# A node's own row in a graph adjacency: summed by products with a unit matrix, or counted into the adjacency itself

## What is computed

```python
# L0: h = x + sum over edges of x[src];  two dense layers, relu
# L1: four times:  h = h @ W;  sum over edges AND the node itself
loop = jnp.arange(n);  src = concatenate([edge_index[0], loop]);  dst = concatenate([edge_index[1], loop])
agg = segment_sum(h[src] * (dinv[src] * dinv[dst])[:, None], dst)
# L2: h = nfeat @ Wn + bn;  msg = edge_norm * (h[src] + e);  agg = segment_sum(msg, dst)
return agg + (h + resid) / degs[:, None]
# L3: twice:  mean over the edges of x[src], without the node itself
agg = segment_sum(x[src], dst) / maximum(cnt, 1.0);  return agg @ W_l.T + b_l + x @ W_r.T
```

## Time and profile before

| | |
|---|---|
| three runs | 2654.14, 2656.84, 2657.05 us; median 2656.84 |
| the profiled execution | 2656.02 us, span 2654.3 us |
| TensorE busy | 2540.9 us, 96% |
| VectorE, ScalarE, GpSimd busy | 1338.1, 613.5, 165.7 us |
| mean granted TensorE clock | 0.993 of full speed |
| building and pass 0's sums | up to about 492 us of the span |
| pass 0's dense layers | up to about 543 us |
| passes 1 to 7 | the rest |

### The profile page before, as it was taken

How to read it: one execution, slowest core, us unless ns; L and a number is a source line. 1 busy time by engine, 2 the same in 40 slices (tenths; PEclk the granted TensorE clock), 3 DMA queues, 4 the chain that set the end, 5 groups by cost and what they waited for, 6 DMA issues and landing times.

```text
span 2654.3 us, 39763 instructions
## 1 busy us (share of the span) xinstructions
PE 2540.9 (96%) x16397; PEld 1530.6 (58%) x16397; DVE 1338.1 (50%) x3515; ACT 613.5 (23%) x742; POOL 165.7 (6%) x113
## 2 busy tenths in 40 slices
PE   1889999789999999999999999999999999999998
PEld 0779999645555555565555655555555555554555
DVE  6877777577878566676666333333222212212222
ACT  2889999530000111111111100000000000000000
POOL 4100000020000111111112000000000200000000
PEclk9999999889999999999999999999999999999999
DMA  5426222347776555555555455445454544455554
GB/s 159 101 83 100 96 96 96 124 127 221 222 221 197 178 182 173 173 175 170 170 170 180 141 180 147 136 132 143 136 136 139 139 139 136 136 139 154 149 153 112
DMA packets 233622, 395.45 MB, mean 149 GB/s; under 512 B 42298, under 2 KB 214158, under 8 KB 229976
## 3 DMA queue, kind: packets, MB, share of 16 engines
q1 hardware_dynamic: 203728, 326.08, 42.9%
q10 hardware_dynamic: 28904, 64.79, 7.4%
q0 software_dynamic: 800, 1.94, 0.2%
HBM read 343.43 MB, written 49.32 MB: 148 GB/s over the span
## 4 chain that ended last, share of the span: by engine, by line
PE 89%; DVE 4%; ACT 2%; DMA 2%; issue 1%; DVEq 1%; POOL 1%; SPq 0%; POOLq 0%; ACTq 0%
PE PS L1601 83%; PE PS L1787 1%; DMA XN<-in_x_dram 1%; PE PS L1794 1%; PE PS L1795 1%; DVE TB L891 1%; PE PS L1809 1%; POOL AT L607 1%; ACT TB L1389 1%; DMA HR<-adjacency 0%; ACT HN L1389 0%; PE PS L1792 0%; PE PS L1818 0%; PE PS L1791 0%; PE PS L1741 0%
## 5 line engine op out<-in xcount | busy, mean ns | idle before, releaser
L1601 PE MATMUL PS<-HR,HN 128*128 128x500 fp8e3 (+1 forms) x5096 | 1062.7, 366 | 4.3 <-DVE HN L1024 2.0
L1601 PE MATMUL PS<-HR,AGN 128*128 128x500 fp8e3 (+1 forms) x4606 | 918.8, 349 | 3.5 <-DMA HR<-adjacency 3.0
L1601 PEld LDWEIGHTS PS<-HR,HN 128*128 128x128 f16 x5096 | 489.5, 97 | 519.3 <-issue 7.8
L1601 PEld LDWEIGHTS PS<-HR,AGN 128*128 128x128 f16 x4606 | 444.5, 97 | 394.7 <-issue 3.5
L1601 PE MATMUL PS<-TB 128*128 128x245 f16 x1250 | 320.4, 275 | 23.2 <-DVE TB L891 22.1
L1102 DVE TENSOR_SCALAR AT<-PS,SC 128x384 f32<-128x384 f32 (+24 forms) x100 | 43.3, 473 | 513.2 <-PE PS L1601 496.6
L891 DVE TENSOR_TENSOR TB<-S,HR 128x1240 f16<-128x1240 f16 x250 | 199.2, 797 | 0.0
L891 DVE TENSOR_TENSOR TB<-iot,HN 128x640 f16<-128x640 f16 x250 | 122.7, 491 | 89.3 <-PE PS L1601 88.6
L1251 DVE TENSOR_SCALAR TB<-iot,dstF 128x208 f16<-128x208 f16 x833 | 159.2, 269 | 5.9
L686 POOL TENSOR_TENSOR AT<-AT,dstI 128x1088 f32<-128x1088 f32 x49 | 100.5, 2051 | 808.6 <-DVE mxe L1225 808.6
L1601 PEld LDWEIGHTS PS<-TB 128*128 128x128 f16 x1250 | 122.1, 100 | 44.9 <-DVE TB L891 19.3
(11 more groups left out here) (243 smaller groups left out, 1846.3 us busy)
## 6 DMA issues: line engine op xcount, KB each, us to landing
HR<-adjacency SPq DMA_DIRECT2D x588, 437.5 KB, 3.5
AT<-source_lanes ACTq DMA_DIRECT2D x49, 544.0 KB, 5.1
AT<-in_edge_attr_dram ACTq DMA_DIRECT2D x48, 544.0 KB, 4.5
adjacency<-HN SPq DMA_DIRECT2D x9, 1531.2 KB, 5.4
adjacency<-HR SPq DMA_DIRECT2D x8, 1531.2 KB, 5.6
adjacency<-TB SPq DMA_DIRECT2D x8, 1531.2 KB, 5.6
HR<-adjacency SPq DMA_DIRECT2D x49, 218.8 KB, 2.5
edge_rows<-AT ACTq DMA_DIRECT2D x8, 416.0 KB
```

The costliest lines, as they stand in the source:

```text
L1601: return t_.matmul(out_, w, m, start=start, stop=True, skip_group_check=True)
```

## The change

VectorE adds the unit matrix to the counts (`diagonal`), in the sub's own blocks, for sub `s` before window 20 of sub `s + 1`, and for the last sub at the end. The store of a sub to memory waits for it (`s_dg`). The products with `U16` fall away in the building and in passes 1 to 4. `sub_pass` takes a sub's own blocks last, and waits for `s_dg` before them. Since every load of the adjacency now holds the node itself, pass 5 gets `h / degs` from its sum: its residual adds only the bias rows that are left, so `second` loses one operation. Passes 6 and 7 subtract the node's row (it stands in `TB`) when VectorE takes the sum out, in place of a plain scaling. The semaphores of the general path are shared by two passes each; that path, which doesn't run here, starts at an in-degree above 39 instead of 40 (the greatest in these inputs is 35).

```diff
-    MOSTDEG = 40
+    MOSTDEG = 39
-    SELF = [0, 1, 2, 3, 4]
+    SELF = [0, 1, 2, 3, 4, 5]
...
-                sp.wait_ge(s_ev, NEV * (s + 1))
+                sp.wait_ge(s_dg, s + 1)
                 sp.dma_start(Ad[s], A16[s % 3]).then_inc(s_aw[s % 3], 16)
...
-            for k in (3, 6):
-                g_.tensor_tensor(BR[:, k, :], BR[:, k, :], BR[:, 2, :], ALU.add)
+            g_.tensor_tensor(BR[:, 6, :], BR[:, 6, :], BR[:, 3, :], ALU.subtract)
+            pool.drain()
+            g_.tensor_tensor(BR[:, 3, :], BR[:, 3, :], BR[:, 2, :], ALU.add)
...
+            def diagonal(s):
+                dve.wait_ge(s_ev, NEV * (s + 1))
+                for b, c0_, d0, w_ in own(SD_ * s, SD_ * (s + 1)):
+                    itself = A16[s % 3][:, SD_ * b + d0:SD_ * b + d0 + w_]
+                    last = v.tensor_tensor(itself, itself, U16[:, c0_:c0_ + w_], ALU.add, saturate=False)
+                last.then_inc(s_dg, 1)
+
             for t in range(NW):
+                if t % SUBW == 20 and t > SUBW:
+                    diagonal(t // SUBW - 1)
...
+            diagonal(NS_ - 1)
...
             def sums(p, u):
-                if p in SELF:
-                    dve.wait_ge(s_agg, idx(p, u) + 1)
-                else:
-                    i = PIECES * u + PIECES - 1
-                    dve.wait_ge(s_af[i % RING], slot_turns(i % RING) * (p - 1) + i // RING + 2)
+                i = PIECES * u + PIECES - 1
+                dve.wait_ge(s_af[i % RING], slot_turns(i % RING) * (p - 1) + i // RING + 2)
                 sums_read(p, u)
+                if p > 5 and u == 0:
+                    dve.wait_ge(s_tb, idx(p - 1, NU - 1) + 1)
...
+                    elif lo < hi and p > 5:
+                        last = v.scalar_tensor_tensor(out=to, in0=y[:, lo - c0:hi - c0], scalar=SC[:, p, 1:2], in1=TB[:, lo:hi],
+                                                      op0=ALU.mult, op1=ALU.subtract)
...
-                v.tensor_tensor(three(t), three(x2), bias(3, n), ALU.add)
-                v.tensor_tensor(three(U5[:, 0:n * P]), three(x2), bias(6, n), ALU.add).then_inc(s_x2f, 1)
+                v.tensor_tensor(three(t), three(x2), bias(3, n), ALU.add).then_inc(s_x2f, 1)
...
-                    v.scalar_tensor_tensor(out=x, in0=U5[:, (b - b0) * P:(b - b0 + 1) * P], scalar=idg[:, b:b + 1], in1=x,
+                    v.scalar_tensor_tensor(out=x, in0=BR[:, 6, :], scalar=idg[:, b:b + 1], in1=x,
                                            op0=ALU.mult, op1=ALU.add)
...
-            def sub_pass(s, k, first=False):
+            def sub_pass(s, i):
+                own_ = [b for b, _, _, _ in own(SD_ * s, SD_ * (s + 1))]
+                k = ([b for b in range(NB) if b not in own_] + own_)[i]
+                if k == own_[0]:
+                    pe.wait_ge(s_dg, s + 1)
...
-            def sub_end(s):
-                for blk_, c0, d0, w_ in own(SD_ * s, SD_ * (s + 1)):
-                    for part in (HI[0], LO[0]):
-                        last = mm(AG2[s % 2][:, d0:d0 + w_], part[:, blk_ * P:(blk_ + 1) * P], U16[:, c0:c0 + w_])
-                last.then_inc(s_un, 1)
...
-                if j == PIECES - 1 and p in SELF:
-                    for blk_, b0_, d0, w_ in own(c0_, c1_):
-                        for part in (hi, lo):
-                            last = mm(y[:, d0:d0 + w_], part[:, blk_ * P:(blk_ + 1) * P], U16[:, b0_:b0_ + w_])
-                    last.then_inc(s_agg, 1)
```

More of the change, by code:

```diff
@@ L221, in build @@
         TT = [[t[:, z + k * MOST:z + (k + 1) * MOST] for k in range(2)] for t, z in ((TB, T14), (AT, o))]
-        U5 = AT[:, o:o + MOST]
         BL = [AT[:, o + k * LW:o + (k + 1) * LW].bitcast(f16) for k in range(2)]
@@ L286, in build @@
         s_stage, s_bc, s_m, s_cmb, s_new = (sem(n) for n in ("staged", "dst_row", "match", "combined", "new"))
-        s_sc = {p: sem(f"scattered_{p}") for p in PASSES}
+        s_sc = [sem(f"scattered_{k}") for k in range(len(PASSES) // 2)]
         s_attr = sem("attr_tile")
@@ L319, in build @@
         s_un = sem("sub_summed")
+        s_dg = sem("nodes_themselves_counted")
         s_aw = [sem(f"sub_stored_{k}") for k in range(3)]
@@ L444, in blk, with scattered @@
             return t[:, :].rearrange("p (b f) -> p b f", f=P)
+        def scattered(p, n):
+            i = PASSES.index(p)
+            return s_sc[i // 2], 16 * (NT * (i % 2) + n)
         flags = {}
@@ L523, in general @@
                 tables(p, h, h if p in SELF else zero)
-                sp.wait_ge(s_sc[p], 16 * NT)
+                sp.wait_ge(*scattered(p, NT))
                 if p == 0:
@@ L538, in _ @@
                 tables("cnt", ones[:, :].unsqueeze(1).to_broadcast(flat), zero)
-                sp.wait_ge(s_sc["cnt"], 16 * NT)
+                sp.wait_ge(*scattered("cnt", NT))
                 with nc.allow_non_contiguous_dma(reason="one word of each row"):
@@ L547, in _ @@
                 tiles(sp, attr_tile)
-                sp.wait_ge(s_sc["attr"], 16 * NT)
+                sp.wait_ge(*scattered("attr", NT))
                 sp.dma_start(Ed[:, :], Gd[:, :]).then_inc(s_dv2, 16)
@@ L645, in tile @@
                                           in_=new, in_offset=None, bounds_check=NP - 1,
-                                          oob_is_err=False).then_inc(s_sc[p], 16)
+                                          oob_is_err=False).then_inc(scattered(p, 0)[0], 16)
                 tiles(pool, tile)
@@ L963, in tile @@
                     v.tensor_tensor(new, PC, old, ALU.add).then_inc(s_new, 1)
-                    dve.wait_ge(s_sc[p], 16 * (t + 1))
+                    dve.wait_ge(*scattered(p, t + 1))
                     dve.sem_inc(s_scrap, 1)
@@ L1624, in _ @@
             pe.wait_ge(s_ct, 1)
-            def sub_pass(s, k, first=False):
+            def sub_pass(s, i):
                 a3 = A16[s % 3].rearrange("p (h c) -> p h c", h=NB)
+                own_ = [b for b, _, _, _ in own(SD_ * s, SD_ * (s + 1))]
+                k = ([b for b in range(NB) if b not in own_] + own_)[i]
+                if k == own_[0]:
+                    pe.wait_ge(s_dg, s + 1)
                 for part in (HI[0], LO[0]):
-                    last = mm(AG2[s % 2], part[:, k * P:(k + 1) * P], a3[:, k, :], start=first and part is HI[0])
-                return last
-            def sub_end(s):
-                for blk_, c0, d0, w_ in own(SD_ * s, SD_ * (s + 1)):
-                    for part in (HI[0], LO[0]):
-                        last = mm(AG2[s % 2][:, d0:d0 + w_], part[:, blk_ * P:(blk_ + 1) * P], U16[:, c0:c0 + w_])
-                last.then_inc(s_un, 1)
+                    last = mm(AG2[s % 2], part[:, k * P:(k + 1) * P], a3[:, k, :], start=i == 0 and part is HI[0])
+                if i == NB - 1:
+                    last.then_inc(s_un, 1)
             LEAD = 4
@@ L1696, in _ @@
                         for k in range(done, NB * (i - LEAD + 1) // (SUBW - LEAD)):
-                            sub_pass(s - 1, k, k == 0)
+                            sub_pass(s - 1, k)
                             done = k + 1
-                if s:
-                    sub_end(s - 1)
             pe.wait_ge(s_ev, NEV * NS_)
@@ L1703, in _ @@
             for k in range(NB):
-                sub_pass(NS_ - 1, k, k == 0)
-            sub_end(NS_ - 1)
+                sub_pass(NS_ - 1, k)
             read_flag(pe, "pe")
```

## The result

The changed kernel took 2637.12 us (median of 4 runs, 2635.13 to 2639.52) against 2656.95 (4 runs, 2654.14 to 2657.16): a ratio of 0.9928, 95% interval 0.9915 to 0.9940. By the medians that is 19.8 us less, where 21.0 were forecast; the forecast time was 2635.0, its range 2631.0 to 2640.5.

The account below looks back on a forecast made before the run. TensorE was taken to bound passes 1 to 4, ScalarE's copies the building's sub ends. Terms 21.6 + 0.25 + 0.5 + 0.45 - 1.8 = 21.0 us, off 2656.0, gave 2635.0 us, range 2631 to 2640.5.

Parts of the forecast that it names:

- Units of the passes: Passes 1 to 4: each removed group of small products at a unit's end frees 0.46 us, 21.6 us in all.
- The first unit of pass 1 and the last units: Pass 1's first unit gains nothing (VectorE's lookup); of four last units, about 0.25 us each, one counts.
- Building, steady: At subs' ends ScalarE's copies set the time; removed products gain nearly nothing, 0.5 us in all; subs stay 16.15 us.
- Additions: VectorE, building: only groups of subs 0, 3 and 4 delay TensorE, 0.51 + 2 x 0.62 = 1.8 us lost.
- SyncE's store comes about ten windows later than now, but its buffer is used again only two subs later: Building: the later store of a sub costs nothing, as its buffer is needed again only 32 us later.
- The building's +2.8 for +1.3: Building and pass 0: forecast to end 1.3 us later net, with 1.8 lost to additions and 0.5 gained.
- Clock: Rival: changed waits add or remove a half-clock stretch, at 130 to 200 us; 2639 or 2631 us, chance 0.04.
- Loads: Rival: loads pace pass 1 and its 5.1 us gain is lost; 2640 us, chance 0.06.
- A load waited for inside a pass: Sign that the forecast is wrong: TensorE waiting for loads within a pass; shortage was expected only at pass starts.
- Pass 5's start, and the second source: Into pass 5, `second`'s removed operation gains 0.45 us; reading a second source in passes 6 and 7 costs nothing.
- The slower rival: Building, window 20: VectorE can't hide additions; gains gone from a 4.6 us group on, 2689 us at 6; chance 0.03.

Follow-up runs that it names:

- the first profile: The changed kernel's profiled execution, with no further edit: 2639.52 us, the longest of its four runs.
- The second profile: The changed kernel run again with no edit: 2635.43 us in the profiled execution, median 2636.86 us, ratio 0.9931.

## Why the prediction was right, and where it was off

**Units of the passes: right.** 0.43 to 0.49 us a unit for the 0.46 forecast, 0.49 to 0.57 in six units of pass 3, and putting zero products back costs 20.6 us for 21.6, net of the clock. The price was the distance of starts and not the busy time, and not ten weight loads either. One unit that was counted in full brought nothing: in the last unit of pass 2 TensorE waits 0.43 us for the sum. The question that was asked of pass 1's first unit, which engine's chain ends there, was not asked there.

**The first unit of pass 1 and the last units: right in kind.** The first brought 0.1, since VectorE's lookup ends the wait. Of pass 1's last unit the load swallowed all. One of the four last units counts, as forecast, but not the one that was meant: pass 2's brought 0.26, since no load is waited for at the start of pass 3, and pass 4's 0.07. There the number was right by luck.

**Building, steady: right.** From the group's old place to the end of the wait for the last copy it is 0.95 us as before, without the group's 0.27; zero products in its place change nothing.

**Additions: the mechanism right, the size too large.** Only the groups of subs 0, 3 and 4 count, as forecast, at 0.40, 0.48 and 0.47 us instead of 0.51, 0.62 and 0.62: 1.35 for 1.8. The three pieces cost less than the 0.11 us each and the 1.16 ns a column that were taken from f32 rows.

**"SyncE's store comes about ten windows later than now, but its buffer is used again only two subs later": the step that was incomplete.** It asked for the buffer and not for what stands behind the store in SyncE's queue. There are the window counts, and VectorE waits for them: 0.68 us in the first profile, 0 in the second. The building's +2.8 for +1.3 is made of that, of 0.34 us of unnamed idle time ahead of `flag`, of 0.56 us at a load's arrival near 75 us, as large as between the two profiles of the kernel before (0.5), and of 0.26 us of the table beside GpSimd's moved addition; the smaller additions take 0.45 off. Together that is 2.7. The `drain` on GpSimd was no term of the sum at all, and its 0.26 are in every profile with the change.

**Clock: the rival happened, in a small way and elsewhere.** It had said that changed waits can add or remove a stretch where TensorE had been waiting; one was added at pass 2's start. Against before, the first unit there falls back by 1.25 us instead of gaining 0.44, so it cost about 1.7. It is in all profiles with the products gone from the passes, and in neither of before nor with zero products back in all four passes. What makes the clock fall there isn't settled, but it isn't the length of the wait: one of 2.41 us (zero products in the building) was followed by the fall, and those of 2.68, 2.68 and 2.71 us (before, twice, and zero products in the passes) weren't.

**Loads: not as a rival had it.** No wait inside pass 1. At the start of pass 4 the load is waited for 0.3 us longer, which swallows pass 3's last unit. In pass 4 the load of the edge sums costs 1.15 us that the prediction did not have, and why it lands later is open. A load waited for inside a pass was on the prediction's own list of signs that it is wrong; this one was too small to take the time out of the range.

**Pass 5's start, and the second source: right.** 0.5 and 0.43 us for 0.45, and nothing in passes 6 and 7.

**The slower rival's point was wrong.** It was put at a group of 4.6 us from 4.1 us of idle time. By the lead of 2.9 us the loss is 20 x (g - 2.9) + 3 x g, which meets 22.8 at g = 3.5. At the real 0.46 us it makes no odds.

Sum over the first profile: 21.0 forecast, less 1.5 in the building, 1.9 in pass 2 (1.7 of clock and the 0.43, less its last unit), 1.1 in pass 4 and 0.6 in pass 1 (0.4 in its first two units, where the two profiles of before differ by 0.67, and 0.2 at its end), is 15.9; 16.5 were measured, with a few tenths regained in passes 3 to 7 and behind the last product. The median is only 2.1 us over the forecast. The second profile, at 2635.43, lacks the two half-clock stretches of the building that before has, so what was missed (some 5 us) and what such stretches gave back (3.5) partly cancel. That the median came so close to the forecast is in part luck.

## What to carry to other kernels

Price a removed product by the distance of starts at its place, and first ask whether another engine's chain sets the end there: 488 of these 634 products were worth 20 us and 146 half a microsecond. When a store gets a new wait, read the whole queue behind it, small transfers too, down to who waits for them. Work moved to an idle engine can slow the busy one beside it: the same additions on GpSimd cost VectorE's tables about what they had cost on VectorE. Whether an engine can hide a burst depends on how far it is ahead at that point, not on its idle time over a period: here 2.9 us against 4.1.

## What the hardware showed beyond that

- An in-place 8-bit addition on VectorE of 128 columns takes 0.20 us to the next start; on GpSimd three of 250 columns in all take 0.90 to 2.90 us.
- A table of 1240 columns on VectorE takes 0.80 us, 0.86 to 1.01 beside an 8-bit addition on GpSimd, and 1.06 beside an f32 addition of 128 columns there.
- VectorE stands 0.42 us with nothing named (0.34 more than before by the starts) ahead of its 320th instruction, in ten profiles; five more instructions in front of the flag's chain move it five places up in that chain.
- A stream on TensorE can stop for 4.58 us with nothing named and nothing changed in its instructions, and the clock is at its lower level for 6.8 us behind it. It was seen in a kernel that leaves VectorE work out, and made that kernel 6 us slower than the one that does it.
- With the products gone, one new half-clock stretch of 3.4 us at the start of pass 2 took back 1.7 of some 20 us gained. The length of the wait before it, 2.41 to 3.56 us, doesn't tell when the clock falls: after 2.71 us it did once and once not.
